# The output projection and the MLP of each group moved into the attention steps of later groups

## The reference

```python
h = _layernorm(x) * g1[:, None, :] + b1[:, None, :]
q, k, v = jnp.split(h @ W_qkv.T + b_qkv, 3, axis=-1)        # 16 heads of 8
scores = jnp.einsum('bhqd,bhkd->bhqk', q, k) / math.sqrt(DH)
attn = jax.nn.softmax(scores, axis=-1)
o = jnp.einsum('bhqk,bhkd->bhqd', attn, v).transpose(0, 2, 1, 3).reshape(B, P, H)
x = res1 + (o @ W_o.T + b_o) * a1[:, None, :]
h = _layernorm(x) * g2[:, None, :] + b2[:, None, :]
h = _gelu_tanh(h @ W_f1.T + b_f1) @ W_f2.T + b_f2           # 128 -> 512 -> 128
x = res2 + h * a2[:, None, :]
```

## Time and profile before

| what | value |
|---|---|
| median of 3 runs | 319.92 us (319.9 to 320.2) |
| the profiled execution: its own time | 319.64 us |
| its span, first to last instruction | 317.8 us |
| TensorE busy | 279.6 us (88%) |
| VectorE busy | 246.6 us (78%) |
| ScalarE busy | 186.3 us (59%) |
| GpSimd busy | 178.6 us (56%) |
| mean granted TensorE clock | 0.983 |

### The profile page before, as it was taken

The page is one execution under the profiler, slowest core; times in us unless marked ns, Lnnn a source line. Parts: engine busy times, 40 slices in busy tenths (PEclk is TensorE's granted clock), DMA queues, the critical chain, the costliest instruction groups (busy, mean ns, idle before and its releaser), DMA issues.

```text
span 317.8 us, 8220 instructions
## 1 busy us (share of the span) xinstructions
PE 279.6 (88%) x2892; PEld 154.6 (49%) x2892; DVE 246.6 (78%) x650; ACT 186.3 (59%) x347; POOL 178.6 (56%) x357
## 2 busy tenths in 40 slices
PE   3989998898989576999999989888877999999993
PEld 2454454454445344555656565655443455555441
DVE  5679997877899976598989898998955676676432
ACT  4557997687768564676677777675545222333330
POOL 8032684985896669377878696953334444322300
PEclk9999999999999997899999999999979999999999
DMA  7940000430340004335354444520000011011112
GB/s 238 327 102 4 0 1 3 120 87 2 92 116 2 0 10 113 86 78 143 93 142 104 119 108 112 149 72 8 6 3 3 0 33 33 1 35 33 33 35 66
DMA packets 26216, 21.57 MB, mean 68 GB/s; under 512 B 4384, under 2 KB 25536, under 8 KB 25920
## 3 DMA queue, kind: packets, MB, share of 16 engines
q1 hardware_dynamic: 25744, 20.37, 24.0%
q10 hardware_dynamic: 432, 0.67, 0.7%
HBM read 4.26 MB, written 2.10 MB: 20 GB/s over the span
## 4 chain that ended last, share of the span: by engine, by line
PE 46%; POOL 20%; DVE 17%; issue 11%; ACT 4%; DMA 1%; POOLq 0%; DVEq 0%; ACTq 0%
PE psum L274 39%; DVE mx L893 5%; POOL q_rest L1016 3%; POOL q_part L1018 3%; POOL q_part L1022 2%; POOL k_rest L1026 2%; DVE hid L838 2%; POOL o_norm L1094 2%; POOL xn_tile L1071 2%; DVE o_turn L900 1%; ACT sq L703 1%; PE psum L623 1%; DVE projT L912 1%; PE psum L460 1%; POOL m_rest L1042 1%
## 5 line engine op out<-in xcount | busy, mean ns | idle before, releaser
L893 DVE TENSOR_REDUCE mx<-psum 128x8 f32<-128x1024 f32 x64 | 75.9, 1193 | 10.5 <-PE psum L274 10.3
L727 ACT ACTIVATE probs<-psum 128x1024 f32<-128x1024 f32 x64 | 65.4, 1023 | 9.5 <-PE psum L274 7.9
L274 PE MATMUL psum<-w_early,h0T 128*128 128x512 f32 x128 | 69.3, 627 | 0.0
L760 ACT ACTIVATE g_act<-psum,w_late 128x512 f32<-128x512 f32 x32 | 22.0, 688 | 46.4 <-PE psum L274 46.4
L274 PE MATMUL psum<-probs,v_pad 128*32 128x128 f32 x1024 | 42.4, 285 | 3.3 <-DVE o_turn L900 2.8
L274 PE MATMUL psum<-h2T,w_late 128*128 128x512 f32 x64 | 31.3, 605 | 0.0
L274 PEld LDWEIGHTS psum<-probs,v_pad 128*32 128x32 f32 x1024 | 25.2, 111 | 11.0 <-ACT probs L727 4.4
L274 PE MATMUL psum<-g_act,w_late 128*128 128x512 f32 x64 | 28.8, 592 | 0.0
L838 DVE SCALAR_TENSOR_TENSOR hid<-psum,rstd,gate 128x512 f32<-128x512 f32 x32 | 23.7, 739 | 6.2 <-PE psum L274 3.7
L695 ACT ACTIVATE gate<-psum,rstd 128x512 f32<-128x512 f32 x32 | 22.0, 688 | 8.9 <-PE psum L274 8.5
L274 PE MATMUL psum<-q_st,k_st 64*128 64x128 bf16 x512 | 26.2, 224 | 0.6 <-DVE mx L893 0.5
(11 more groups left out here) (125 smaller groups left out, 541.3 us busy)
## 6 DMA issues: line engine op xcount, KB each, us to landing
q_st<-q_part SPq DMA_DIRECT2D x48, 128.0 KB
k_st<-k_part SPq DMA_DIRECT2D x48, 128.0 KB, 2.4
x_tok<-x SPq DMA_DIRECT2D x8, 256.0 KB, 7.2
out<-out_t SPq DMA_DIRECT2D x8, 256.0 KB, 2.3
w_late<-late SPq DMA_DIRECT2D x1, 1159.5 KB, 9.1
w_early<-early ACTq DMA_DIRECT2D x2, 256.0 KB, 5.4
k_st<-k_st SPq DMA_DIRECT2D x4, 128.0 KB, 4.9
q_st<-q_st SPq DMA_DIRECT2D x4, 128.0 KB
```

Of the source, the lines that this page charges most:

```text
L274: return nc.tensor.matmul(o, w, m, start=start, stop=stop, skip_group_check=shares)
L727: nc.scalar.activation(probs[:, n % 3, :, :, :].rearrange("p f j q -> p (f j q)"), psum[:, pair[0]:pair[1] + 1, :].rearrange("p a b -> p ( ...
L760: nc.scalar.activation(g_act[:, f, :], bank(2 + f % 2), ACT.Gelu_apprx_tanh, bias=wl("b_f1")[:, f:f + 1]).then_inc(c_gelu[f], 1)
L893: v.tensor_reduce(mx[:, c % 2, :, r, :], psum[:, pair[0]:pair[1] + 1, :].rearrange("p f (j k) -> p f j k", j=4), X_AXIS, ALU.max, negate=T ...
```

## The change

The last part is gone. Its pieces are units that stand in the attention steps of later groups, and the loop over steps runs on to step 40 (`LAST_STEP`). With `LAG`, group `g` has its output projection in step 4g+5, the residual in 4g+6, the layer norm on GpSimd in 4g+7, its transposes and the four `up` in 4g+8, the `down` of chunks 0 and 1 in 4g+9, of 2 in 4g+10, of 3 in 4g+11, and the last transposes and addition in 4g+12. From step 7 on (`TWO_PAIRS`) the exponential's scores have only pair 0 and the maxima's scores only pair 1; banks 5 and 6, the third pair, hold `up` chunks 0 and 2 (`UP_BANK`) and the accumulation and the last transposes (`DOWN_BANK`). `up` chunks 1 and 3, the projection, the residual and the norm share bank 7. ScalarE loads the gelu table ahead of each group's four gelus and the exp table behind them. The k projection moves from the first step of a group to the end of the step before.

```diff
+UP_BANK, DOWN_BANK = 5, 6
...
-    name, ahead = {3: ("q", 9), 0: ("k", 8), 2: ("v", 2)}.get(b % GRP, (None, 0))
+    names, ahead = {3: ("qk", 9), 2: ("v", 2)}.get(b % GRP, ("", 0))
...
-FRONT = {27: ("proj", 0), 28: ("res", 0), 29: ("proj", 1), 30: ("norm", 0)}
-FRONT_END = {30: ("res", 1)}
+LAST_STEP = 4 * (NG + 2)
+LAG = dict(proj=(1, 1), res=(2, 1), norm=(0, 2), up=(0, 2), down1=(1, 2), down2=(2, 2), down3=(3, 2), y=(0, 3))
+
+TWO_PAIRS = 7
...
+    def fill_pair(kind, b, r, step):
+        n = len(pairs)
+        pairs.append((kind, b, r))
+        if step >= TWO_PAIRS:
+            owner.append(0 if kind == "exp" else 1)
+        else:
+            owner.append(n % 2 if n < 2 * LEAD else n % 3)
...
+            def up(g, f):
+                if f == 0:
+                    pe.wait_ge(c_h2T, g + 1)
+                if f % 2:
+                    shared_free("up", (g, f))
+                elif f == 2:
+                    pe.wait_ge(c_gelu[0], g + 1)
...
+                mm(bank(MISC_BANK if f % 2 else UP_BANK), wl("f1")[:, f * P:(f + 1) * P], h2T[:, :]).then_inc(c_f1_mm[f], 1)
+
+            def down(g, f):
+                pe.wait_ge(c_gelu[f], g + 1)
+                if f == 0 and g:
+                    pe.wait_ge(c_out, g)
+                last = mm(bank(DOWN_BANK), wl("f2")[:, f * D:(f + 1) * D], g_act[:, f, :], f == 0, f == FC - 1)
...
+                if unit("up", b) is not None:
+                    if b <= B:
+                        nc.scalar.activation(warm[:, :], zero_c[:, :], ACT.Gelu_apprx_tanh)
+                    gelus(unit("up", b))
+                    if b + 1 < B:
+                        nc.scalar.activation(warm[:, :], zero_c[:, :], ACT.Exp)
...
             def attention(b):
+                pre = 0 <= b + LEAD < B
                 if 0 <= b - 1 < B:
                     normalize(b - 1)
-                if 0 <= b + LEAD < B:
+                if unit("norm", b) is not None:
+                    modulate(unit("norm", b))
+                if pre:
                     maxima(b + LEAD, 0)
...
-            for i in range(2, NG + 3):
-                mlp(i)
```

More of the change, by code:

```diff
@@ L88, in numbered, with unit @@
+LAST_STEP = 4 * (NG + 2)
+LAG = dict(proj=(1, 1), res=(2, 1), norm=(0, 2), up=(0, 2), down1=(1, 2), down2=(2, 2), down3=(3, 2), y=(0, 3))
+TWO_PAIRS = 7
+def unit(kind, b):
+    place, behind = LAG[kind]
+    g = b // GRP - behind
+    return g if b % GRP == place and 0 <= g < NG else None
 def numbered():
     shared, pairs, owner = [], [], []
+    def fill_pair(kind, b, r, step):
[5 more added lines that the diff above has]
+            owner.append(n % 2 if n < 2 * LEAD else n % 3)
@@ L102, in attention @@
[L102 to L105, removed]
-        if pre:
-            pairs.append(("max", b + LEAD, 1))
-        if b in FRONT_END:
-            shared.append(FRONT_END[b])
+            fill_pair("max", b + LEAD, 0, b)
+        if unit("proj", b) is not None:
+            shared.append(("proj", unit("proj", b)))
+        if unit("res", b) is not None:
+            shared.append(("res", unit("res", b)))
@@ new lines, in attention @@
+        shared.extend(p for p in late_proj(b) if p[0] == "q")
+        if on:
+            fill_pair("exp", b, 1, b)
+        if 0 <= c < B and b % GRP == 0:
+            shared.append(("m", c))
+        if pre:
+            fill_pair("max", b + LEAD, 1, b)
+        if 0 <= c < B and b % GRP:
+            shared.append(("m", c))
+        shared.extend(p for p in late_proj(b) if p[0] != "q")
+        if unit("up", b) is not None:
+            shared.extend([("up", (unit("up", b), f)) for f in (1, 3)])
@@ L360, in _ @@
                         third_k(g)
-            for g in range(NG):
-                sp.wait_ge(c_out, g + 1)
-                sp.dma_start(out_d[:, g * GRP:(g + 1) * GRP, :], out_t[:, :, :]).then_inc(stored, 16)
+                if unit("y", b - 1) is not None:
+                    store(unit("y", b - 1))
+            for b in range(B, LAST_STEP + 2):
+                if unit("y", b - 1) is not None:
+                    store(unit("y", b - 1))
             sp.wait_ge(stored, 16 * NG)
@@ new lines, in down, with y_tokens @@
+            def down(g, f):
[3 more added lines that the diff above has]
+                last = mm(bank(DOWN_BANK), wl("f2")[:, f * D:(f + 1) * D], g_act[:, f, :], f == 0, f == FC - 1)
+                if f == FC - 1:
+                    last.then_inc(c_f2_mm, 1)
+            def y_tokens(g):
+                pe.wait_ge(c_yT, g + 1)
+                for s in range(GRP):
+                    last = nc.tensor.transpose(bank(DOWN_BANK)[:, s * P:(s + 1) * P], yT[:, s, :], eye)
+                last.then_inc(c_y_mm, 1)
@@ L729, in exps, with gelus @@
                                      scale=DH ** -0.5).then_inc(b_exp, 1)
+            def gelus(g):
+                for f in range(FC):
+                    act.wait_ge(c_f1_mm[f], g + 1)
+                    if f == 0 and g:
+                        act.wait_ge(c_f2_mm, g)
+                    nc.scalar.activation(g_act[:, f, :], bank(MISC_BANK if f % 2 else UP_BANK), ACT.Gelu_apprx_tanh,
+                                         bias=wl("b_f1")[:, f:f + 1]).then_inc(c_gelu[f], 1)
             def attention(b):
@@ L750, in _ @@
                     attention(s - B_AT)
[L751 removed]
+            for b in range(A_STEPS - B_AT, LAST_STEP + 1):
                 attention(b)
[L753 to L761 removed]
         @block.vector
```

240 lines of the change are left out of this document (100 added, 140 removed).

## The result

The changed kernel takes 353.01 us (median of 4 runs, 352.29 to 354.15), against 319.91 for the kernel before in the same comparison (4 runs): a ratio of 1.104 with a 95% interval of 1.101 to 1.107. It is slower, by 33 us. Throughout, a run more than 1.5% above the fastest of its kernel is left out of times and ratios (two of four in e2, one of four in e3, whose profile is of that run, and one of the kernel before). The profiled execution has an own time of 352.81 and a span of 350.3, against 317.8.

A forecast was written before the change was run, and what follows sets the result against it. TensorE was taken as the bound, nearly full in the attention and alone in the last part. Terms 156 + 83.4 + 25.8 + 27.2 + 23.4 + 33.3 gave 349.1 us of span, forecast 350 us, range 336 to 362.

The forecast's parts named there:

- steps 8 to 19: Three full groups of four attention steps with the moved units, 27.8 us each: 83.4 us.
- steps 20 to 27: Two groups of attention steps: 25.8 us for steps 20 to 23, without q and k, and 27.2 for 24 to 27.
- Up to step 8: Start of the span to step 8: waits for bank 7 and the gate, a k moved ahead; step 8 starts 6.8 us later.
- The work of a group: TensorE's work in four steps after the change, without waits: 24.4 us, against 24.0 before.
- (b): Rival: f32 matmuls keep 0.86 us and transposes 0.44 among small items, saving 2.2 us a group; 3 in 100.
- The waits of a group: TensorE's added waits in a full group, for modulation, gelu, bank 7 and maxima pair: 3.4 us, giving 27.8 a group.
- The table switch: ScalarE's gelu and exp table loads, two a group: 1.40 us each from load start to next instruction.
- The end: Stretch with no attention beside it, groups 6 and 7, including 3.6 us of TensorE idle for the layer norm: 33.3 us.
- (a): Rival: the added waits do not come, 321 us; half of them, 340 us, 16 in 100; none, 2 in 100.
- (c): Rival: TensorE's clock falls once in each of six groups, 1.7 us a group, 360 us or above; 17 in 100.
- (d): Rival: the change does nothing of note, since units are few beside the 90 us of attention; 1 in 100.
- The third pair: Score pairs in the attention: losing one adds waits of 0.1 and 0.4 us in a group's second and third step.

The follow-up runs named there:

- e2: Changed kernel with each gelu table load ahead of, not behind, the copy of the maxima: 346.17 and 348.79 us, ratio 1.090.
- e3: Changed kernel with the identity in place of the gelu and no table load in the attention steps: 346.55 us, ratio 1.086.
- e1: Kernel before, with only the pairs dealt out as in the change (from step 7 exponential pair 0, maxima pair 1), nothing moved: 331.88 us, ratio 1.040.
- the five kernels named above: The changed kernel, e2, e3, e4 and e6, which have the same instructions up to the copy of `m_T` in step 3; copy at 136.4 to 141.8 us.
- e10: Changed kernel with the edits of e2, e4, e5, e6 and e9 together: 339.73 us, ratio 1.062.
- e5: Changed kernel with the maxima's transpose ahead of the second maxima scores in the third and fourth step of each group too: 354.08 us, ratio 1.110.
- e9: e5 plus VectorE's scaling of `yT` ahead of the second maxima of the group's fourth step: 349.4 us, ratio 1.092.
- e4: Changed kernel with four unread f32 matmuls in TensorE's wait for the last group's layer norm: 351.14 us, ratio 1.103.
- e6: Changed kernel with `down` 1 directly behind `down` 0 instead of alone behind the weighting: 354.66 us, ratio 1.111.
- e8: Kernel before, with four unread f32 matmuls of 256 columns ahead of the maxima's transpose in steps 1 and 29: 318.45 us, ratio 0.996.

## Why the prediction was right

**The time.** I forecast 350 us and 349.1 of span; measured are 353.01 and 350.3. The mechanism held: no group got cheaper in TensorE's own work, and waits of TensorE came on top, in the places that I had named. The sum, term by term:

| term | predicted | measured |
|---|---|---|
| first score matmul of step 8 | 156.0 | 156.8 |
| steps 8 to 19 | 83.4 | 82.4 |
| steps 20 to 27 | 53.0 | 52.1 |
| steps 28 to 31 | 23.4 | 22.5 |
| from there to the end | 33.3 | 36.5 |
| span | 349.1 | 350.3 |
| own time less span | 1.8 | 2.5 |

That the span is off by only 1.2 us is in part luck: start and end are 4.0 us too short together, the three terms of groups 2.8 too long.

**Up to step 8.** I added 6.8 us and 7.6 were measured. From the copy in step 3 on it is 5.7 (20.4 against 14.7), with a wait of 1.30 for the gate in step 5 where I had 1.7. The other 1.9 lie ahead of that copy, and none of my steps has them. The k projection of group 2 moves too, into step -1, and meets two waits there. The v projection has moved as well, in every group, which neither my list of the change nor this term has: before it stands in the middle of its step (125.91, without a wait), now behind `transpose_max` of step 2. TensorE's timeline of the changed kernel, k first, then v:

```profile
113.71 1.10 PE L297 MATMUL psum<-feat,wk_h 128*128 128x512 f32 x2 [0.44 <-ACT m_T L776]
...
115.68 0.45 PE L650 MATMUL psum<-w_first,xn_tile 128*128 128x128 f32 x1 [0.87 <-ACT k_f L707]
...
130.40 1.13 PE L297 MATMUL psum<-w_late,feat 128*128 128x128 f32 x8 [0.44 <-ACT m_T L776]
132.29 0.30 PE L650 MATMUL psum<-w_first,xn_tile 128*128 128x128 f32 x1 [0.77 <-ACT v_pad L698]
```

Before, neither k nor v stood here, and the waits of 0.87 and 0.77 for their copies out of PSUM weren't there, together 1.6 us where 1.9 are to be explained. The windows of the changed kernel behind it have a clock of 0.67 and 0.50 already:

```profile
114.00:118.00 4.00, 2.86 (x32) 1.58 (x34) 1.56 (x4) 2.44 (x4) 0.83 (x4) 0.67 0.04 8
118.00:122.00 4.00, 4.00 (x60) 2.45 (x54) 2.25 (x4) 2.39 (x4) 3.07 (x4) 0.50 0.09 23
```

Before, 120 to 124 was the first with less than 1 (0.81). But e1, whose k and v stand in the old places, had a clock of 0.50 all through 112 to 124 as well, and has its copy at 134.3 us all the same, while the five kernels named above have theirs at 136.4 to 141.8. So the low clock alone doesn't delay that copy; this speaks for the moved k and v as the cause. Neither was tried alone.

**The work of a group.** I summed 24.4 us without waits; TensorE was busy 24.80. The term that is short is "`up` 1 to 3 in a row 2.78": in the kernel they don't stand in a row, since the wait for `g_act` divides them, and took 3.04 us (189.53 to 193.54 less the wait of 0.97); even in a row they took 2.96 (e10). The projection with `down` 0 took 2.05, where I had 1.92. The 1.06 us of a lone f32 matmul, on which rival (b) turned, is as I read it. That the filled holes are paid back in slower matmuls is what e10 shows with the waits gone.

**The waits of a group.** I had 3.4 us (those that I list add to 3.3), the trace shows 2.6. The order is mine: `g_act` 0.97 (1.1), `v` and `k` 0.44 each (0.45), `h2T` 0.47 (0.7), `mx` 0.25 (0.4). The waits of 0.1 for `up` 1 and in the second step aren't there. The two errors, work 0.4 too short and waits 0.8 too long, partly cancel: 27.8 predicted, 27.45 measured. e2 took the `g_act` wait away and gained 0.96 of a group, which settles that this one alone was worth about 6 us in all. e5 and e9 settle `v` and `k`: worth 0.66 a group, once VectorE's line ahead of `up` 0 is shortened too.

**The table switch.** I charged 1.40 us from the start of the load and not the 2.66 of the Trainium skill (ScalarE: Activation LUTs, What ACT_TABLE_LOAD costs). The trace shows 1.40 and 1.41 (189.50 to 190.90, 194.35 to 195.76) and no further drain, as before. The Trainium skill's advice to do all of one set before switching held in sign: without any load the stretch was 8.0 us shorter (e3). But 6.4 of these came back with both loads kept and the first one moved into a wait of ScalarE (e2), and its price per switch isn't what these rows show.

**The end.** This is the term that was mis-sized, 33.3 against 36.5. From the last norm's transposes to the scaling of `yT` I had 27.5 - 17.6 = 9.9 us; the trace has 344.80 - 332.07 = 12.73. Of the 9.9, 2.5 were for the clock and 7.4 for the work. The windows show 0.50 for eight us behind the wait of 3.74, longer than the dip of the earlier trace rows, from which I had sized it, and e4 gave 3.2 us back by filling the wait. So the clock was 0.7 short. The larger part lies in the chain itself: at a clock of 1.00 e4 still takes 9.48 between the same two instructions, 2.1 more than my 7.4, and a wait of 1.02 for the modulation is in it.

**The rivals.** (a), no waits, would need groups near 24.4; 27.45 were measured, and even e10 has 25.5. (b) fell with the 1.06. (c) fell: the clock is 1.00 in each window of the groups, with waits of 0.5 and 1.0 us in them. (d) fell.

**The third pair.** I charged its loss with 0.5 us a group, the waits of 0.1 and 0.4 in the second and third step; 0.25 is left in the trace. e1 says that it costs the attention 2.3 us a group when nothing stands between the fills. My small term was right because the units do stand there, which I hadn't written down.

**Where the 30.6 us of the stretch went.** TensorE's busy time there rose from 166.2 to 179.2 (13.0) and its idle time from 17.0 to 34.7 (17.7). With all mends (e10) the stretch is still 16.1 above the kernel before. Less the 3.6 us of filling matmuls, its busy time is 173.3, 7.1 above, and the idle or filled time 26.0, 9.0 above. Of these 26.0, 14.2 lie in the last 40 us (29.39 busy, 3.6 of it filling), where the last groups run one behind the other with little attention beside them; before, the rounds of three or four groups overlapped there, and only 4.9 us of the last 40 were idle:

```profile
277.80:317.80 40.00, 35.12 (x110) 16.49 (x108) 20.31 (x63) 11.00 (x16) 7.22 (x9) 0.99 0.14 40
```

The difference, 9.3, is as much as the 9.0 us of idle time that no mend took away. That last share is read from the windows; no experiment of its own was made for it.

## What to carry to other kernels

Before moving work into the holes of another loop, compare what the bound engine does with it in both places: a train of eight large matmuls ran at 0.88 us each, the same ones alone or in twos and threes between small items took 0.91 to 1.06, and that with the transposes cost more than the holes of 1.03 us a group were worth. Count the holes of the engine that the moved work needs, not the share of the span that the removed part had: here TensorE was 93% busy in the place that was to take in 9.2 us a group. And when a step in the middle of such a chain is mended, look for the engine that is next in line; e5 lost two thirds of its gain to VectorE until e9 moved one instruction.

## What the runs showed that I had not expected

- The low clock of TensorE varies from run to run of the same instructions. In the early part the copy of `m_T` in step 3 came between 136.4 us (clock 1.00 from 130 on in the changed kernel's profile) and 141.8 (0.50 in 128 to 140 in that of e6) over five profiles. This moves the whole time by more than some edits do. Behind the 3.74 us of wait at the end the clock was 0.50 for eight us and 0.83 in the next two.
- Where a wait was filled with matmuls that nobody reads, the clock was 1.00 there and in the eight us behind (e4, e8). It doesn't keep the clock from falling elsewhere (e8, 108 to 116).
- The same k cast on VectorE took 0.68 us before, 1.15 in the full groups of the changed kernel and 1.64 in e1, where GpSimd works beside it. In e1 its delay went straight into a wait of 1.21 us of TensorE. What lengthened it wasn't tried.
